# Moving one intermediate tensor through four buffers, in longer rows, by one queue, and splitting it on GpSimd

## The reference

```python
t1 = einsum('nchw,he->ncew', gn(x), p1)                 # h (32) becomes e (16)
t3 = depthwise_conv(t1, p3)                             # 9x9, one filter per channel
t4 = grouped_conv(t3, p4)                               # groups of 4 channels, 5x1
t5 = einsum('ncew,ewf->ncf', t4, p5)                    # contracts e and w
t6 = depthwise_conv(t5, p6)                             # 3 taps along f
out = einsum('ncf,nfp->ncp', t6, t2) / sqrt(3 * c)      # t2: three row-shifted copies of gn(x)
x = x + out
```

## Time and profile before

| what | us |
|---|---|
| median of 3 runs | 372.99 |
| lowest and highest of the 3 | 367.62, 376.11 |
| the profiled execution | 367.42 |
| its span, first to last instruction | 365.5 |
| around the span (the difference) | 1.9 |

### The profile page before, as it was taken

How to read it: one execution, slowest core, us unless ns; L and a number is a source line. 1 busy time by engine, 2 the same in 40 slices (tenths; PEclk the granted TensorE clock), 3 DMA queues, 4 the chain that set the end, 5 groups by cost and what they waited for, 6 DMA issues and landing times.

```text
span 365.5 us, 4713 instructions
## 1 busy us (share of the span) xinstructions
PE 289.2 (79%) x1560; PEld 233.3 (64%) x1560; DVE 294.2 (81%) x539; ACT 215.3 (59%) x317; POOL 182.7 (50%) x186
## 2 busy tenths in 40 slices
PE   4566759999894994999989999999999999873000
PEld 0000129999783994567778888888888888651000
DVE  4899977985891862357668999999999999979792
ACT  3444665665963854364565667776676666530891
POOL 7454670050440040302487888888888888842000
PEclk9999998999999896999999999999999999995555
DMA  7979814589359761589000000000000000000399
GB/s 187 245 186 237 239 44 131 175 264 273 109 136 312 256 166 35 134 320 385 3 2 0 2 0 2 2 0 0 2 1 2 0 2 2 0 0 1 154 402 363
DMA packets 18344, 43.59 MB, mean 119 GB/s; under 512 B 2992, under 2 KB 7344, under 8 KB 18320
## 3 DMA queue, kind: packets, MB, share of 16 engines
q1 hardware_dynamic: 16928, 41.00, 36.6%
q0 software_dynamic: 960, 2.09, 2.3%
q10 hardware_dynamic: 432, 0.21, 0.2%
HBM read 30.44 MB, written 8.39 MB: 106 GB/s over the span
## 4 chain that ended last, share of the span: by engine, by line
DVE 48%; PE 21%; issue 8%; DMA 7%; SPq 6%; ACT 6%; POOL 3%; DVEq 0%; POOLq 0%; ACTq 0%
PE wide L637 10%; DVE xa L770 5%; DVE st L878 5%; DMA d_sb<-t_out 5%; DVE x_sb L983 4%; DVE x_sb L871 4%; DVE y_sb L917 4%; SPq L276 4%; DVE sty L923 3%; DVE sty L759 3%; DVE d_split L784 2%; DVE y_sb L910 2%; DVE u_sb L854 2%; DVE u_sb L846 2%; DVE u_sb L863 2%
## 5 line engine op out<-in xcount | busy, mean ns | idle before, releaser
L637 PE MATMUL wide<-t_all,s_hi 128*128 128x272 f32 x320 | 50.2, 306 | 15.5 <-ACT s_hi L465 12.9
L637 PEld LDWEIGHTS wide<-t_all,s_hi 128*128 128x128 f32 x320 | 45.2, 202 | 18.4 <-ACT s_hi L465 14.6
L778 DVE TENSOR_TENSOR s_lo<-s_f,s_hi 128x768 fp32r<-128x768 f32 x32 | 32.1, 1002 | 24.9 <-ACT s_hi L465 24.8
L429 POOL TENSOR_TENSOR g_lo<-y_sb,g_hi 128x1024 fp32r<-128x1024 f32 x15 | 36.2, 2411 | 14.4 <-ACT y_sb L562 14.4
L561 ACT ACTIVATE g_hi<-x_sb,rs 128x1024 fp32r<-128x1024 f32 x16 | 21.4, 1340 | 33.8 <-POOL rs L414 33.8
L607 PE MATMUL bank<-xa,p_blk 128*64 128x512 f32 x64 | 28.2, 979 | 14.8 <-DVE xa L770 14.8
L233 PE MATMUL wide<-g_hi,t_hi 128*128 128x512 f32 x96 | 38.0, 395 | 0.7 <-DVE t_lo L898 0.7
L276 POOL DMA_DIRECT2D d_sb<-t_out x24 | 13.3, 560 | 50.3 <-ACT t_out L479 43.9
L235 PE MATMUL wide<-g_hi,t_lo 128*128 128x512 f32 x96 | 37.7, 393 | 0.0
L234 PE MATMUL wide<-g_lo,t_hi 128*128 128x512 f32 x96 | 37.7, 392 | 0.0
L770 DVE STREAM_TRANSPOSE xa<-x_slot 128x1024 f32<-128x1024 f32 x16 | 31.6, 1993 | 6.6 <-DMA x_slot<-in_x 6.3
(11 more groups left out here) (130 smaller groups left out, 815.8 us busy)
## 6 DMA issues: line engine op xcount, KB each, us to landing
s_f<-in_taps SPq DMA_DIRECT2D x32, 384.0 KB, 4.8
x_sb<-in_x SPq DMA_DIRECT2D x8, 1024.0 KB, 7.8
x_slot<-in_x SPq DMA_DIRECT2D x28, 256.0 KB, 5.4
out<-x_sb SPq DMA_DIRECT2D x7, 1024.0 KB, 5.0
d_sb<-t_out POOLq DMA_DIRECT2D x24, 68.0 KB, 4.4
d_sb<-t_out SPq DMA_DIRECT2D x24, 68.0 KB, 5.1
x_slot<-in_x SPq DMA_DIRECT2D x8, 128.0 KB, 2.8
out<-x_sb SPq DMA_DIRECT2D x2, 512.0 KB, 2.7
```

The lines of the kernel that those rows point to most:

```text
L429: pool.tensor_tensor(g2_lo[:, :], y_sb[:, n, :], g2_hi[:, :].bitcast(F32), ALU.subtract).then_inc(s["g2_lo"], 1)
L637: mm = pe.matmul(ps_t3[g % 2], weights[:, g % SR, 128 * t:128 * t + 128], t1_all[:, (2 * g + part) * JP + t:(2 * g + part) * JP + t + J, : ...
L778: dve.tensor_tensor(s_lo[:, g % SR, :], s_f[:, g % WR, :], s_hi[:, g % SR, :].bitcast(F32), ALU.subtract).then_inc(s["s_lo"], 1)
```

## The change

There are four d buffers now, d_sb0 to d_sb3, laid where t1 lay, above p5_hi and p5_lo; p5_raw stands above d_sb0. A buffer may be written when PE has left that part of t1: 12, 15, 19 and 22 groups done for the four, by their sizes, instead of "DVE has read the batch before". The same shift puts p5_raw higher, and `p5_groups` comes out as 12 instead of 8. Within t4_out and d the order of axes is now such that a block's row on a partition is one piece of 2176 bytes, where it was four of 544. SP issues all 16 blocks of batches 0 to 2, four in a step; for the last batch SP has six, POOL five, ACT five. POOL splits all four quarters of batches 0 and 1, two of batch 2 and one of batch 3 (a copy and a subtraction each); ACT and DVE keep five quarters, behind the loop. POOL's power stands behind the split of batch 0, and what DVE does with its result in step 27. x returns from SP behind the last batch-2 block: images 0 and 1 before the end of the loop, 2 and 3 behind the last batch's blocks, all others when all of d is split; the load of the second block's weights moves ahead of the last batch's blocks.

```diff
-AGGR_AT, ST1_AT, GST_AT = 8, 12, 15
+AGGR_AT, ST1_AT, GST_AT, RS1_AT = 8, 12, 15, 27
 SHUFFLE_AT = (14, 22, 30)
-SP_BLOCKS = 8
-RELOAD_AT = (27, 28)
-D_AT = (14, 22, 29)
+PER_STEP = 4
+LAST_SP, LAST_POOL = 6, 5
+BY_POOL = (4, 4, 2, 1)
...
         at_x = cursor[0]
+        d_sb = [put("d_sb0", [CI, GB, JC, NO])]
         p5_raw = put("p5_raw", [JC, NF])
         end_raw = cursor[0]
+        ends_d = [end_raw]
+        for b in range(1, NB):
+            d_sb.append(put(f"d_sb{b}", [CI, GB, JC, NO]))
+            ends_d.append(cursor[0])
...
         p5_groups = groups_below(end_raw)
+        d_groups = [groups_below(end) for end in ends_d]
+        x_groups = groups_below(at_x + 4 * HW * 2)
...
-        t4_out = put("t4_out", [2, JL, JC, GB, NO])
+        t4_out = put("t4_out", [2, JL, GB, JC, NO])
...
                 eng.dma_start(
-                    d_of(b)[32 * jl:32 * jl + 32, :, co, :, :].rearrange("p j g n -> p j (g n)"),
-                    t4_out[32 * co:32 * co + 32, b % 2, jl].rearrange("p j g n -> p j (g n)")
+                    d_sb[b][32 * jl:32 * jl + 32, co].rearrange("p g j n -> p (g j n)"),
+                    t4_out[32 * co:32 * co + 32, b % 2, jl].rearrange("p g j n -> p (g j n)")
                     ).then_inc(done, 16)
...
             eng.wait_ge(s["t4_ev"], GB * (b + 1))
-            if b == 0:
-                eng.wait_ge(s["x_used"], 2 * N)
-            elif b < NB - 1:
-                eng.wait_ge(s["d_lo"], b)
+            eng.wait_ge(s["conv"], d_groups[b])
...
-                    i = 2 * (step - SHUFFLE_AT[b])
+                    i = PER_STEP * (step - SHUFFLE_AT[b])
                     if i == 0:
                         d_ready(sp, b)
-                    if 0 <= i < SP_BLOCKS:
-                        shuffle(sp, b, blocks[i:i + 2], d_in[b])
+                    if 0 <= i < len(blocks):
+                        shuffle(sp, b, blocks[i:i + PER_STEP], d_in[b])
...
+            sp.wait_ge(s["d_pool"], BY_POOL[0])
+            sp.wait_ge(s["conv"], x_groups)
+            reload_x(sp, 0)
+            sp.wait_ge(s["x_used"], 2 * N)
+            sp.dma_start(w_raw[:, :, :], w_in).then_inc(s["w_raw"], 16)
             d_ready(sp, NB - 1)
-            shuffle(sp, NB - 1, blocks[:7], d_in[NB - 1])
+            shuffle(sp, NB - 1, blocks[:LAST_SP], d_in[NB - 1])
             sp.wait_ge(s["conv"], G)
...
+            sp.wait_ge(s["p5_lo"], JC)
+            sp.wait_ge(s["d_pool"], BY_POOL[0] + BY_POOL[1])
+            reload_x(sp, 1)
+            sp.wait_ge(s["d_pool"], sum(BY_POOL))
+            sp.wait_ge(s["d_lo"], CI * NB - sum(BY_POOL))
+            for k in range(2, N // 2):
                 reload_x(sp, k)
...
+            def d_split_pieces(b, pieces):
+
+                wait_d(pool, b)
+                if b == 0:
+                    pool.wait_ge(s["x_used"], 2 * N)
+                for co in pieces:
+                    src, hi, lo = split_views(b, co)
+                    link(pool.tensor_copy(hi, src))
+                    pool.tensor_tensor(lo, src, hi.bitcast(F32), ALU.subtract).then_inc(s["d_pool"], 1)
+
+            d_split_pieces(0, range(BY_POOL[0]))
+            pool.wait_ge(s["gst"], 1)
+            pool.tensor_tensor(rs1[:, 1, :], rs1[:, 0, :], minus_half[:, :].broadcast_to([128, N]),
+                               ALU.pow).then_inc(s["gst_q"], 1)
+            d_split_pieces(1, range(BY_POOL[1]))
+            d_split_pieces(2, range(BY_POOL[2]))
+            d_ready(pool, NB - 1)
+            shuffle(pool, NB - 1, blocks[LAST_SP:LAST_SP + LAST_POOL], d_in_pool)
...
+            d_split_pieces(3, range(CI - BY_POOL[3], CI))
...
-                for b in range(NB - 1):
-                    if D_AT[b] <= g < D_AT[b] + JC:
-                        d_high(b, g - D_AT[b])
...
-            shuffle(act, NB - 1, blocks[13:], d_in[NB - 1])
...
+            shuffle(act, NB - 1, blocks[LAST_SP + LAST_POOL:], d_in[NB - 1])
+            for co in range(BY_POOL[2], CI):
+                d_high(2, co)
+            for co in range(CI - BY_POOL[3]):
+                d_high(3, co)
```

More of the change, by code:

```diff
@@ L205, in build @@
         d_in = [sem(f"s_d_in{b}") for b in range(NB)]
-        d_in_pool = [sem(f"s_d_in_pool{b}") for b in range(NB)]
+        d_in_pool = sem("s_d_in_pool")
         s_in = [sem(f"s_s_in{r}") for r in range(WR)]
@@ L268, in wait_d @@
         def wait_d(eng, b):
-            by_pool = JL * CI - SP_BLOCKS if b < NB - 1 else 6
-            eng.wait_ge(d_in[b], 16 * (JL * CI - by_pool))
-            eng.wait_ge(d_in_pool[b], 16 * by_pool)
+            if b < NB - 1:
+                eng.wait_ge(d_in[b], 16 * len(blocks))
+            else:
+                eng.wait_ge(d_in[b], 16 * (len(blocks) - LAST_POOL))
+                eng.wait_ge(d_in_pool, 16 * LAST_POOL)
         def shuffle(eng, b, some, done):
```

78 lines of the change are left out of this document (22 added, 56 removed).

## The result

The changed kernel takes 366.47 us (median of 20 runs, 364.52 to 371.15) where the kernel before, beside it on the same chips, takes 371.51 (20 runs, 367.62 to 376.11). The ratio, which leaves out the three runs of the changed kernel that lay over 1.5% above its fastest, is 0.9876, 95% interval 0.9847 to 0.9905: 4.6 us faster. I had forecast 356.0, with a range from 348 to 365, so the time is 1.5 us outside. The sign is right, the size is not: it is under the 2% that I had called no change, to which I had given 0.12.

The account below looks back on a forecast made before the run. Two limits on t5: PE's loop plus 13.06 us, and d being ready. d ready at 146.5 put t5 at 146.6, not 160.68: 14.1 off 365.5 is 351.4, plus 1.9 and 2.8 gives 356; range 348 to 365.

Parts of the forecast that it names:

- The frame: Start of t5: set by PE's loop plus 13.06 us of products or by d being ready; the same program behind it.
- 2.0 (p5): PE's loop: 2.0 us lost to taps late behind p5 and SP's four-block steps, ends 0 and 6.4.
- 2.5 (GpSimd and DVE): PE's loop: 2.5 us lost as DVE's two-input instructions and POOL's exclude each other, ends 0 and 6.
- At the taps' 0.33 a step is 1.7 and costs nothing ... so I take the second.: SP's queue: a block costs 0.33 us, not 0.7, so steps of four blocks delay no taps.
- the longer rows bring nothing: Rival, SP's queue: a block still costs 0.7, batch 0's steps add 2.7, t5 at 149.3, 358.8 us; chance 0.13.
- Directly behind p5 I take 5.4, so 87.1, and a stall of 1.9.: Group 14: its taps, issued behind p5, land 5.4 us after issue, at 87.1, and stall 1.9 us.
- About 1 in each of two steps where DVE has p5's remainder too.: PE's loop: s_lo beside GpSimd costs about 1 us in each of two steps with p5's remainder.
- costed at nothing: Put at zero: quarters taken from ACT and DVE, the load of weights, the reload of images 0 and 1.
- GpSimd is the bound: Rival, d's split: the copy costs as much as the subtraction, 4.9 us a quarter in the loop, 364.3 us; chance 0.17.
- Ports kept: Rival, loop: s_lo gets no turn until a batch is through, PE stops, t5 at 170.5, 380 us; chance 0.03.
- leaves SP near 124: SP's queue: reload of images 0 and 1 issued near 124, with until 132.4, 8 us against 5.4 needed.
- plus 1: Last batch: POOL's blocks land 1 us later for the reload of x that SP issues among them, at 141.3.

Follow-up runs that it names:

- e10: Kernel before with only the new axis order in t4_out, d_sb and d_last (rows of 2176 bytes); 369.98 us, ratio 0.995.
- e6: Changed kernel with three blocks a step on SP instead of four; 364.46 us, ratio 0.978.
- e4: Changed kernel with DVE's normalisation factors in step 22 instead of 27; 366.91 us, ratio 0.985.
- e3: e2 with p5 split in steps 12 to 16 instead of 15 to 19, before GpSimd begins with d; 359.94 us, ratio 0.964.
- e9: Changed kernel with factors at step 31, images 0 and 1 reloaded ahead of batch 2's last eight blocks, 2 and 3 after d's split; 368.09 us, ratio 0.989.
- e11: e8 with images 0 and 1 reloaded ahead of the last eight of SP's blocks of batch 2; 354.06 us, ratio 0.955.
- e1: Changed kernel with GpSimd's copy and subtraction of d replaced by two memsets that read nothing; 362.38 us, ratio 0.972.
- e2: Changed kernel with the places of p5_raw and batch 0's buffer exchanged, so p5 waits for 8 groups, not 12; 364.42 us, ratio 0.975.
- e5: e2 with the blocks of batch 0 starting in SP's step 16 instead of 14; 360.76 us, ratio 0.970.
- e7: Changed kernel with DVE's normalisation factors in step 31 instead of 27; 365.91 us, ratio 0.984.
- e8: Changed kernel: e2's exchange, p5 split from step 12, batch 0 blocks from 16, factors at 31, images 2 and 3 later, last batch without GpSimd; 355.11 us, 0.953.

## Why the prediction was wrong

**The frame held.** t5 starts one product time behind the loop: 14.2 us in the forecast (132.4 to 146.6), 14.0 in the result (144.31 to 158.30). The waits of ACT for d are gone, the limit on d came out 0.8 us behind the products, and nothing behind t5 differs. The forecast of the loop's end was 11.9 us early and that of t5 11.7, so the error is ahead of the loop's end: the terms 2.0 (p5) and 2.5 (GpSimd and DVE), and one that was missing, stood where 16.4 us were lost. It is in four steps.

**"At the taps' 0.33 a step is 1.7 and costs nothing ... so I take the second."** Wrong, and against the rows: 0.7 a block stood in the earlier trace rows for this very transfer. It is 0.6 to 0.7 with 32 rows (the changed kernel, e10) and 0.6 to 0.7 with 128 (the kernel before). The price on the queue hardly follows the rows; that it must I had reasoned from one other transfer. For PE at group 17 it mattered little (0.2 us in e6); it helped to make batch 0 late at GpSimd and, with twelve blocks in a row, the reload of x. Rival "the longer rows bring nothing" was right in its premise, as e10 showed, and had 0.13.

**"Directly behind p5 I take 5.4, so 87.1, and a stall of 1.9."** The taps landed 6.6 after issue, behind p5 on busy DMA engines (share 0.99 to 1.05), and PE stopped for 2.87. And I had left out what the slow clock adds, which I had read for the stalls of before: ten matmuls at 2.63 and ten at 2.25 against 1.42, 2.8 us with those behind them. The term is 6.1 where I had 2.0; its upper end of 6.4, reached by other terms, held it. In e4 the clock did not fall (granted 1.00 from 88 to 104 us) and PE was as late at group 17 (6.1), by three more stops for taps (0.67, 0.97, 0.54): the two costs hide each other.

**"About 1 in each of two steps where DVE has p5's remainder too."** It was 1.2 to 1.4 in each of four steps, 5.5 in all with 0.1 for the step before. I had let the exclusion fit into 1.2 us of slack, which it does for s_lo alone: 0.4 us in the seven steps from 22 to 29, about the 0.5 that the 2.5 left for it. I had not laid p_lo, s_lo, copy and subtraction end to end. That sum is 4.3 against a step of 2.26, from prices that I had to within 0.3, and would have shown that these steps can't be hidden. e3 takes p_lo away, and all but one of the steps with it.

**The factors were "costed at nothing" by silence.** I asked when DVE gets POOL's power and not what DVE's five small instructions cost beside GpSimd: 4.2 us instead of 0.9, and 3.9 on PE's path with the slow clock. The rule I had drawn, that an instruction with two SBUF inputs is held, was too narrow: the one-input L825 and L827 are held too. e4, e9 and e11 each put them where GpSimd reads nothing, and each has 0.17 to 0.22, 0.17 and 0.51 there; e1, with memsets, has 0.17, 0.58 and 0.51. What the collision costs PE hangs on when GpSimd's instructions fall: with the factors in the same step it was 1.8 us in e2, 2.0 in e5, 3.6 in e3 and 5.0 in e6.

**What of GpSimd was right.** A quarter took 3.67 in batch 0, where p_lo set the pace, and 3.53 on average in batch 1 (forecast 3.75), the power 3.64, the subtraction 1.7 alone (1.64). The copy took 1.14, where I had taken 0.9, and 0.07 to 0.09 lay between it and the subtraction (0.1, which no row of before shows). "GpSimd is the bound" fell: it waited 46.1, 2.9, 5.1 and 3.3 us for blocks. Batch 0 was done at 114.1 instead of 110.3 because SP's blocks were late (landed at 99.66 and not 95.3), and batches 1 and 2 because PE's loop was. The rival with 0.03, in which s_lo gets no turn until a batch is through, fell too: DVE got its turn after each single instruction (s_lo was over 0.81 us after the subtraction at 101.33). "Ports kept", as the chances call it, is only a name: no run shows ports.

**Costed too low and hidden by the rest.** The reload of images 0 and 1 "leaves SP near 124"; it left at 138.31, behind twelve blocks at 0.7. It was just in time in the changed kernel, whose loop ended at 144.3. For my forecast loop, over at 132.4, it would have been late. So even with the right loop t5 would have come some microseconds behind the forecast: e1, e4 and e7 show it, and e8 and e11 what undoing it takes. That the last blocks took 6.3 us from POOL's first issue, where the forecast's terms make 6.2, is luck: without the reload they take 4.3, so the landing was costed 0.9 too high, and the "plus 1" for the reload was 2.0 (up to 5.4 in e1). And from landing to d ready it was 6.3 us and not 5.2: DVE's last three subtractions took 4.91 beside POOL's own quarter, 3.75 in e1.

With these collisions undone, e8 comes to what I had forecast for the changed kernel: t5 at 146.84 against my 146.6, and 355.1 us. The frame bears that out, but that the numbers meet so closely is in part luck: e8 is another kernel, its loop ended 2.1 us earlier than my 132.4, and its products waited 1.63 us for x.
